# First layer's experts: ScalarE casts the last two parts of the coming expert's weights before it evicts the block's outputs

## The reference, cut to what matters

```python
def _moe_forward(x, gate_w, wg, wu, wd):          # E, I, K = (8, 1024, 2)
    logits = x_flat @ gate_w.T
    top_v, top_i = jax.lax.top_k(logits, K)
    probs = jax.nn.softmax(top_v.astype(jnp.float32), axis=-1)
    ...
    def body(acc, ws):
        wge, wue, wde, we = ws
        hidden = jax.nn.silu(x_flat @ wge.T) * (x_flat @ wue.T)
        return (acc + we[:, None] * (hidden @ wde.T), None)
```

## Time and profile before

| | |
|---|---|
| median of 3 runs | 921.59 us (919.04 to 923.31) |
| the profiled execution's own time | 923.3 us |
| its span, first to last instruction | 921.6 us |
| PE, DVE, ACT, POOL busy | 77%, 61%, 44%, 32% of the span |
| mean granted TensorE clock | 0.879 |

### The profile page before, as it was taken

How to read it: one execution, slowest core, us unless ns; L and a number is a source line. 1 busy time by engine, 2 the same in 40 slices (tenths; PEclk the granted TensorE clock), 3 DMA queues, 4 the chain that set the end, 5 groups by cost and what they waited for, 6 DMA issues and landing times.

```text
span 921.6 us, 19114 instructions
## 1 busy us (share of the span) xinstructions
PE 708.8 (77%) x6266; PEld 552.5 (60%) x6278; DVE 560.0 (61%) x1396; ACT 403.0 (44%) x720; POOL 293.2 (32%) x285
## 2 busy tenths in 40 slices
PE   5676786987744999998997989995762098889882
PEld 4223454554534898887885878895441076767771
DVE  7778586887653645564645646457687445566441
ACT  1135465766430635463545535443443045445331
POOL 6415201416258213122212122121045414333342
PEclk8788898978666999999998999997755589999996
DMA  4661303302336523534535523415023455464332
GB/s 134 122 138 39 58 1 62 135 23 77 118 112 234 149 44 63 145 76 127 126 77 152 143 63 94 107 26 174 23 79 111 160 166 125 103 149 118 54 58 39
DMA packets 68419, 92.25 MB, mean 100 GB/s; under 512 B 14442, under 2 KB 54435, under 8 KB 68348
## 3 DMA queue, kind: packets, MB, share of 16 engines
q1 hardware_dynamic: 41788, 63.37, 23.2%
q0 software_dynamic: 14592, 16.24, 10.4%
q10 hardware_dynamic: 11968, 11.72, 4.9%
HBM read 64.21 MB, written 29.87 MB: 102 GB/s over the span
## 4 chain that ended last, share of the span: by engine, by line
PE 42%; DVE 26%; issue 13%; ACT 8%; DMA 4%; ACTq 2%; POOL 2%; another core or an unknown queue 1%; DVEq 1%; POOLq 0%; SPq 0%
PE ps L659 40%; DVE probs L1690 2%; DVE stats L1357 2%; DVE mx L1553 2%; DVE keys L1768 2%; DVE probs L1773 2%; ACT probs L1163 1%; DMA out_x<-keys,row_to 1%; DMA probs<-rows 1%; POOL rows L612 1%; DVE keys L1747 1%; ACT expo L1160 1%; ACT probs L1241 1%; ACT probs L1245 1%
## 5 line engine op out<-in xcount | busy, mean ns | idle before, releaser
L1768 DVE TENSOR_TENSOR keys<-probs,ps 128x512 f32<-128x512 f32 x122 | 82.7, 686 | 191.6 <-PE ps L659 121.8
L659 PE MATMUL ps<-keys,slot 128*128 128x256 f16 (+1 forms) x1440 | 149.5, 266 | 15.5 <-issue 8.9
L659 PE MATMUL ps<-keys,probs 128*128 128x256 f16 (+1 forms) x1488 | 139.9, 255 | 19.2 <-issue 15.6
L659 PEld LDWEIGHTS ps<-keys,slot 128*128 128x128 f16 x1440 | 128.5, 100 | 35.6 <-issue 17.5
L659 PEld LDWEIGHTS ps<-keys,probs 128*128 128x128 f16 x1488 | 123.6, 98 | 34.6 <-issue 19.9
L575 POOL DMA_INDIRECT attended<-keys,row_to x42 | 68.9, 1641 | 167.6 <-ACT keys L1253 145.4
L1241 ACT ACTIVATE probs<-ps 128x512 f32<-128x512 f32 x122 | 71.4, 598 | 79.9 <-PE ps L659 75.3
L1253 ACT ACTIVATE keys<-ps,carried 128x256 f32<-128x256 f32 x80 | 33.5, 470 | 150.4 <-issue 84.4
L1245 ACT CAST probs<-keys 128x512 f16<-128x512 f32 x122 | 74.8, 614 | 26.8 <-DVE keys L1768 24.2
L1773 DVE TENSOR_TENSOR probs<-keys,probs 128x512 f16<-128x512 f32 x122 | 83.5, 688 | 3.8 <-ACT probs L1245 2.0
L1690 DVE TENSOR_TENSOR probs<-expo,probs 128x512 f16<-128x512 f32 x80 | 61.8, 784 | 33.1 <-ACT probs L1163 29.7
(11 more groups left out here) (277 smaller groups left out, 1147.6 us busy)
## 6 DMA issues: line engine op xcount, KB each, us to landing
inbox<-in_W SPq DMA_DIRECT2D x24, 512.0 KB
probs<-rows ACTq DMA_DIRECT2D x44, 260.0 KB
inbox<-in_wg SPq DMA_DIRECT2D x16, 512.0 KB
inbox<-in_wu SPq DMA_DIRECT2D x16, 512.0 KB, 3.8
inbox<-in_wd SPq DMA_DIRECT2D x16, 512.0 KB, 4.2
rows<-zeros SPq DMA_DIRECT2D x16, 260.0 KB
x<-in_x SPq DMA_DIRECT2D x4, 512.0 KB, 6.3
q_out<-queries SPq DMA_DIRECT2D x8, 256.0 KB, 2.1
```

Source lines behind the costliest of these rows:

```text
L659: return pe.matmul(o, l, r, start=start, stop=stop, **kw)
L1768: dve.tensor_tensor(h32[:, j % 2, :], s_act[:, j % 2, :], ps[:, 2 * (j % 2) + 1, :], ALU.mult).then_inc(S(r + "_h32"), 1)
```

## The change: the last two casts go ahead of the eviction

For the first layer ACT casts part 4 in the fourth step, right behind part 3, and part 5 after it has started the load of block g+2 and before it waits for the end of down. The order on DVE (`low_beside`) stays as it was, and so does every other instruction. In the second layer the fifth entry of `beside` is empty, so that moving `split(pairs)` changes nothing there.

```diff
-            l.beside = (([0], [1], [2], [3], [4, 5]), ([0], [1, 2], []))[n]
+            l.beside = (([0], [1], [2], [3, 4], [5]), ([0], [1, 2], []))[n]
             l.low_beside = (([0], [1], [2], [3], [4, 5]), ([0], [], [1, 2]))[n]
...
                     act.wait_ge(S(r + "_xbT_ps"), g + 3)
                     act.wait_ge(S(r + "_carried"), g + 2)
                     load(g + 2)
+                    split(pairs)
                     act.wait_ge(S(r + "_down"), g + 2)
                     wait_counted(act, S(r + "_added"), g + 1)
                     for hf in range(2):
                         ins = act.activation(yb[:, hf, :], ps[:, 4 + hf, 0:D], ACT.Identity, ...)
                     ins.then_inc(S(r + "_y"), 1)
-                    split(pairs)
```

## The result

The changed kernel takes 914.47 us (median of 6 runs, 912.04 to 914.94); the kernel before 921.44 us (median of 6, 919.04 to 926.4). The ratio is 0.990, 95% interval 0.9873 to 0.9927: about 9 us faster (the medians alone differ by 7.0 us, and the interval runs from 6.7 to 11.7), where the prediction said 5.8 us from a range that ended at 9.1. A second measurement of the same two kernels gave 0.9877 (0.9849 to 0.9904), some 11 us.

The account below looks back on a forecast made before the run. PE was taken as the bound, stalling on late weight casts before pair 2 and before expert 5. Gains of 3.7 + 2.1 = 5.8 us take the median of 921.6 to 915.8 us; range 912.5 to 920.8.

Parts of the forecast that it names:

- 1.5 us left: Upper end of the range, 920.8 us: the stalls-move case with 1.5 us left of its gain, less scatter.
- Kind A: First blocks of experts 0, 1, 2, 3, 5, 6: PE's stalls for DVE's product before pair 2; 3.7 us removed.
- The six stalls are the 4.1 us of the earlier trace: PE's six waits for DVE's product (L1768) total 4.1 us of idle time, the starting size of the stall saving.
- experts 3 and 5 keep 0.17 and 0.27 us: Stall left before pair 2 in these experts' first blocks, because part 5 lands late; 0.44 us off the gain.
- Kind B: Expert 4's single block: PE's 6.56 us idle before expert 5, partly waiting for weights; 2.1 us removed, 4.4 left.
- The clock: PE's lower clock level after the idle time before expert 5: 1.6 us lost on 96 matmuls, left as it is.
- The stalls move: Rival: eviction and ACT's queue become what is late for pair 2; gain only 2.5 us, 919.1 us; chance 0.27.
- slower: Rival: part 5 lands much later, so ACT holds eviction and Silu longer; 7 us slower, 928.6 us; chance 0.06.

Follow-up runs that it names:

- the extra cast: Changed kernel plus one unused 1.04 us cast ahead of part 5's cast in each first block of the first layer; ratio to the kernel before 0.992 (0.9898 to 0.9942).
- the two profiles with the load moved: Kernel before and changed kernel, each with the load of block g+2's rows behind the eviction in the first layer; ratios to the kernel before 1.003 and 0.9956.
- the late fetch: Changed kernel with SP fetching part 5 only when part 3, not part 2, is finished; ratio to the kernel before 0.9982 (0.9961 to 1.0003).
- the four buffers: Changed kernel with four staging buffers instead of three and both casts in the fourth step, first layer; ratio to the kernel before 0.9888 (0.9857 to 0.9919).

## Why the prediction was wrong

The mechanism was right, and the size of the gain was not: 5.8 us was forecast, and the ratio says 9.2 (6.7 to 11.7). The median of 914.47 us lies within the range of 912.5 to 920.8 (whose upper end is 919.1 plus 1.7 us of scatter; the "1.5 us left" named for it does not give it), but the ratio applied to the 921.6 us from which the forecast started gives 912.4, just below it.

*Kind A's size is the first step that failed: 3.7 us in the sum, 5.2 us measured.* "The six stalls are the 4.1 us of the earlier trace rows" took the idle column for the loss. But the 48 matmuls ahead of a stall are given 5.40 us, with the modelled end of the last, and where PE runs on, the next 48 start 5.24 us after their first. A stall of 0.67 us is 378.89 - 372.81 - 5.24 = 0.84 us of time. The blocks' lengths show it without that trap: 17.02 against 16.17 us. Six times 0.86 are 5.2 us, 1.1 more than the 4.1 us that the term started from.

*The step "experts 3 and 5 keep 0.17 and 0.27 us" failed too.* The path from the cast of part 5 to the product's end measured 3.17 us (371.89 to 375.06; 3.5 in expert 6), not 3.66: the eviction follows the cast with no step, and so does Silu the eviction. The product ended at G+4.16 to G+4.66 in the six blocks. PE wants its end by about G+5.2 and not G+5.36 (the next 48 matmuls start at G+5.24, and the extra cast shows G+5.19 to be in time), by the same mistake as above, but the path is 0.49 us shorter, and no stall was left. The landings were 3.6 to 4.5 us; but with the 4.9 and 5.0 us that the prediction took for experts 3 and 5 the measured path would have ended in time as well, at G+5.04 and G+5.14. Both together make kind A 5.2 instead of 3.7 us.

*Kind B.* Forecast 2.1 us, idle time 4.4 us left; measured 1.8, 1.9 and 2.2 us less than the mean before, 4.73, 4.62 and 4.37 left. Right, within 0.4 us. Its length fell by 2.2 us.

*The clock.* The loss of 1.6 us stayed, as taken. But the argument for it, idle time of 4.4 us being nearer to 4.1 than to 3.3, was no argument, and that it came out is luck: at expert 5 the clock fell behind 2.71 us, and before expert 3 it stayed up behind 3.29 and 3.10 us and fell behind 3.00, 3.08, 3.14, 3.15 and 3.18. Behind 1.63 to 2.50 us there it never fell (6 profiles).

*What no term of the sum held* is the change into expert 3: 0.8 us less idle time in the mean of three profiles and 1.0 us less lost to the clock. The prediction used that idle time of 3.29 us only as a bound for another place, as if it were fixed. It is not fixed: PE starts 2.8 to 3.0 us after a packet of the instruction queue, wherever that falls. That much is read from 13 profiles; that PE waits for the packet is the likely reading, and no run moved the packet alone. That the load of rows holds the packet up is supported by the two profiles with the load moved and by where the late packets lie, and the first of those two met only a part of what was expected. It is not shown. Why the packet was ahead of the load in some profiles of the changed kernel and never in three of the kernel before stays open, and with three profiles of each kernel, and one of the changed kernel's (3.00 us) near those before, so does whether the change moves it at all. About 7.1 us (5.2 + 1.9 of idle time before expert 5) are there in every profile; the other 2 to 4 us of the two ratios are left for this and the clock, by subtraction.

*The rivals.* "The stalls move" did not happen with the landings as they are (3.6 to 4.5 us in the kernel after). It and "slower" describe the same bound, which the late fetch brought out: 1.7 us later, and the gain is all but gone. The break-even worked out there, a landing of 5.4 us for kind A, was half a us too early: from the measured path and bound it is G + 5.19 - 3.17 + 0.85 = G+2.87, a landing of 5.9 us. With the issue 1.7 us later, part 5 landed 3.5 to 5.0 us after it, 4.0 in the mean of the six blocks; that is 5.8 us after the old issue, and 5.0 of the 5.2 us were given back. The rule that the prediction took from the Trainium skill's page "DMA: Bandwidth & Descriptors", section "Rules for kernel authors", names the right risk: ACT's idle time ended by in_wd is 23.7 us over the stretch in the kernel after, about 1.7 us for each of 14 parts, and there was none before. The rule does not say who waits behind it. In the six blocks of kind A nobody on PE's path did, and that time cost nothing. In kind B PE did: the four buffers show 1.1 to 1.5 us of it.

## What to carry to other kernels

A wait moved ahead of other work on an in-order engine is free as long as its end lies before the point from which the consumer's deadline is counted back. Work out that point and the landing's scatter, because 1.7 us of later landing undid nearly all of it here. Size a stall by the spacing of the same work with and without it (block length, or start to start), not by the idle column, when the engine's ends are modelled. Where a gap is ended by "issue", look at the instruction queue's packets, and at a second profile, before treating its length as a constant.

## What the runs showed of the hardware that I had not expected

PE started expert 3's code 2.8 to 3.0 us after a packet of the instruction queue, in 13 of 14 profiles, with gaps of 1.6 to 3.3 us by where the packet fell, and went on 2.2 to 2.9 us after one inside experts 2 and 6, in all 14. The lower clock level came behind gaps of 2.7 us at one place and not behind 3.3 us at another; where it came, the next 96 matmuls took 12.2 to 13.6 us instead of 10.65, so that one such gap moves an execution by 1.5 to 2.9 us, as much as two or three of the stalls that the change removed.
